# A Fourier network, windowed attention and a mixture of experts on one core: gate work moved between the expert products, and the last two spectra copied apart

## What is computed

```python
# tokens: 32 images, 64x64 pixels, 3 colours
x = coords @ fc0_w + fc0_b
for sw, cw, cb in four_layers:                       # 20 x 20 modes, 32 channels
    x1 = irfft2(einsum(rfft2(x)[:20, :20], sw))      # spectral part
    x = gelu(x1 + einsum(x, cw) + cb)                # pointwise part
h = gelu(x @ fc1_w + fc1_b) @ fc2_w + fc2_b          # (32, 64, 64)
h = concat([cls_tok, h])                             # 65 tokens of width 64
h = h + attention(layernorm(h))                      # 8 heads, window of 32
y = layernorm(h)                                     # "second norm" below
logits = y @ gate_w.T                                # 64 experts
top, idx = top_k(logits, 6); scores = softmax(top)
lattice = sum_k scores_k * (y @ lattice_weights[idx_k])
h = h + layernorm(y + lattice @ out_w.T + out_b) * ln_g + ln_b
```

## Time and profile before

| | us |
|---|---|
| median of 3 runs | 1065.15 (1063.59 to 1070.08) |
| the profiled execution's own time | 1065.44 |
| its span in the profile | 1063.6 |
| PE busy in the span | 962.6 (91%) |
| DVE busy in the span | 613.7 (58%) |

### The profile page before, as it was taken

How to read it: one execution, slowest core, us unless ns; L and a number is a source line. 1 busy time by engine, 2 the same in 40 slices (tenths; PEclk the granted TensorE clock), 3 DMA queues, 4 the chain that set the end, 5 groups by cost and what they waited for, 6 DMA issues and landing times.

```text
span 1063.6 us, 36547 instructions
## 1 busy us (share of the span) xinstructions
PE 962.6 (91%) x17004; PEld 619.0 (58%) x17004; DVE 613.7 (58%) x771; ACT 397.5 (37%) x524; POOL 152.4 (14%) x160
## 2 busy tenths in 40 slices
PE   4899999989989998999899999989888799678896
PEld 3576666656756633566567657657415587633343
DVE  2267457726844322477358548733244577768997
ACT  1333323233223387232233323223695567421200
POOL 6000000000000000000000000020000575325432
PEclk9999999999999999999999999999999899869999
DMA  6220131022011400410220031020011000000000
GB/s 197 97 79 3 40 109 30 4 94 80 3 65 49 143 5 12 121 50 3 95 80 3 15 122 40 3 95 18 2 24 47 1 2 2 1 1 1 1 7 16
DMA packets 25931, 46.78 MB, mean 44 GB/s; under 512 B 9962, under 2 KB 11013, under 8 KB 25138
## 3 DMA queue, kind: packets, MB, share of 16 engines
q1 hardware_dynamic: 24131, 42.47, 12.9%
q0 software_dynamic: 1456, 1.63, 0.6%
q10 hardware_dynamic: 192, 0.33, 0.1%
HBM read 30.25 MB, written 10.89 MB: 39 GB/s over the span
## 4 chain that ended last, share of the span: by engine, by line
PE 71%; DVE 13%; issue 5%; ACT 4%; DMA 2%; POOL 2%; SPq 1%; DVEq 0%; POOLq 0%
PE PSALL L1363 22%; PE PSALL L1331 8%; PE PSALL L1222 5%; PE PSALL L1354 5%; PE PSALL L1306 4%; PE PSALL L1236 4%; PE PSALL L550 3%; DVE WORK L1577 3%; PE PSALL L449 3%; DVE WORK L1064 2%; PE PSALL L1421 2%; DVE WORK L1596 2%; PE PSALL L536 2%; PE PSALL L1199 2%; PE PSALL L1350 2%
## 5 line engine op out<-in xcount | busy, mean ns | idle before, releaser
L1596 DVE STREAM_TRANSPOSE WORK<-PSALL 128x1024 f32<-128x1024 f32 x128 | 152.5, 1230 | 251.4 <-PE PSALL L1331 251.4
L1363 PEld LDWEIGHTS PSALL<-EW,WORK 128*64 128x64 f32 x4096 | 221.8, 138 | 72.8 <-issue 48.3
L1363 PE MATMUL PSALL<-EW,WORK 128*64 128x128 f32 x4096 | 247.6, 276 | 14.0 <-DVE WORK L1596 13.8
L1496 ACT ACTIVATE X<-PSALL,TABLES 128x1024 f32<-128x1024 f32 x128 | 141.8, 1114 | 306.5 <-PE PSALL L1363 306.5
L1577 DVE STREAM_TRANSPOSE WORK<-PSALL 128x1024 f32<-128x1024 f32 x84 | 104.3, 1242 | 32.7 <-PE PSALL L1222 30.9
L347 POOL DMA_DIRECT2D WORK<-MIXED x32 | 17.6, 550 | 666.0 <-ACT MIXED L1487 555.6
L1478 ACT COPY SPEC<-PSALL 128x400 f32<-128x400 f32 x64 | 54.0, 850 | 139.1 <-PE PSALL L1236 132.8
L1236 PEld LDWEIGHTS PSALL<-TABLES,WORK 128*64 128x64 f32 x2000 | 67.5, 139 | 47.4 <-DVE WORK L1577 31.4
L1064 DVE TENSOR_TENSOR WORK<-PSALL,X 128x910 f32<-128x910 f32 (+1 forms) x80 | 79.4, 1018 | 16.0 <-PE PSALL L536 14.4
L1236 PE MATMUL PSALL<-TABLES,WORK 128*64 128x64 f32 x2000 | 81.1, 228 | 7.5 <-DVE WORK L1577 3.9
L1530 ACT ACTIVATE WORK<-PSALL,B 128x1024 f32<-128x1024 f32 x64 | 68.2, 1114 | 8.3 <-PE PSALL L1421 7.3
(11 more groups left out here) (165 smaller groups left out, 1150.4 us busy)
## 6 DMA issues: line engine op xcount, KB each, us to landing
SW<-in_spec_w SPq DMA_DIRECT2D x160, 80.0 KB, 2.7
spec_scr<-MIXED SPq DMA_DIRECT2D x24, 400.0 KB, 3.2
SPEC<-spec_scr SPq DMA_DIRECT2D x32, 200.0 KB
WORK<-spec_scr SPq DMA_DIRECT2D x16, 200.0 KB
WORK<-in_coords_w SPq DMA_DIRECT2D x2, 1024.0 KB, 4.8
XC<-in_coords_c SPq DMA_DIRECT2D x2, 1024.0 KB, 7.1
WORK<-MIXED SPq DMA_DIRECT2D x40, 40.0 KB
WORK<-MIXED POOLq DMA_DIRECT2D x32, 40.0 KB
```

The source lines that it names most:

```text
L1363: m = pe.matmul(PS[2 * p + z][64 * j:64 * j + 64, 2 * b * GRID:(2 * b + 2) * GRID], G[:, n % 2, b, h:h + 2, :, t].rearrange("p q o -> p (q ...
L1496: nc.scalar.activation(X[:, n].rearrange("p b (z d) c w -> p d z b (c w)", z=2)[:, p, :, :, 2 * t * GRID:2 * (t + 1) * GRID], PSALL[:, 2 * ...
L1596: nc.vector.transpose(G[:, n % 2, 2 * x + y].rearrange("p h o v -> p o h v"), PSALL[:, 4 + 2 * x:6 + 2 * x, :].rearrange("p k (h o v) -> p ...
```

## The change

It has two parts that don't touch.

**The tail.** The loop has 44 steps in place of 52. Gate rows and logits of chunks 2 and 3 stay at steps 34 and 38 but go through bank 7 (before: banks 0 and 1), so rows of chunk 2 and 3 now wait for the residual that reads bank 7; those of chunks 4 to 7 stand in the expert stage after pairs 3, 5, 15 and 18 (logits one pair later). The second norm of block 2 stops at its centring (step 31); its variance stands at step 41 and its last three steps at pairs 0 and 1. The norm of block 3 starts at steps 42 and 43 and goes on at pairs 3, 4, 7 and 8. Both score chunks of block 0 are turned at step 41, each into a pair of banks of its own; `low_part(1)` goes from POOL to the DVE. PARTS3 moves to other memory and LG's blocks are rotated by one, for room. Ten products that nothing reads (`SPARE_PRODUCTS`, 128x512, bank 5) stand in PE's program: one each at steps 37, 38 and 39, two at 40 and five at 41, behind the score rows. The deviation (ACT's square root) of block 2 stands at step 41, that of block 3 behind the logits of chunk 5.

**The forward parts.** In each of the six, the eighth copy is split. Image 14's spectrum goes to one bank and is copied by ACT (`last_spectrum`, 128x200) while image 15 is still on its way; image 15's goes to the other bank and is copied by the DVE (128x200). `rows` of image 15 waits for the copy of round 6, which frees that bank; `mix()` waits for both.

The diff, cut to its core:

```diff
-ROWS_AT, CHOICE_AT, PARTS_AT = 26, 32, 40
-TAIL_STEPS = 52
+ROWS_AT, CHOICE_AT, PARTS_AT = 26, 32, 41
+TAIL_STEPS = 44
+ROWS_PAIRS = [3, 5, 15, 18]
+for i, k, s in ((29, 2, 0), (30, 2, 1), (31, 2, 2), (41, 2, 5), (41, 2, 6), (42, 3, 0), (43, 3, 1), (43, 3, 2)):
+    NORM_STEPS.setdefault(i, []).append((k, s))
+NORM_PAIRS = {0: [(2, 8), (2, 9)], 1: [(2, 10)], 3: [(3, 5)], 4: [(3, 6)], 7: [(3, 8), (3, 9)], 8: [(3, 10)]}
+SPARE_PRODUCTS = {37: 1, 38: 1, 39: 1, 40: 2, 41: 5}
...
             def gate_rows(c):
-                if c == 0:
-                    pe.wait_ge(pj_ready, (ROWS_AT - 5) // BC)
...
+                if c < 4:
+                    pe.wait_ge(pj_ready, (ROWS_AT - 5) // BC + c)
+                elif c == 4:
+                    pe.wait_ge(pj_ready, NC)
+                    pe.wait_ge(o_ready, NC)
+                elif c == 6:
+                    pe.wait_ge(rest_ready, 4)
...
-                        pe.wait_ge(lg_ready, min((i - ROWS_AT) // BC + 1, 2))
+                        pe.wait_ge(lg_ready, min((i - ROWS_AT) // BC + 1, 4))
...
-                if i in (PARTS_AT, PARTS_AT + 2):
-                    score_rows((i - PARTS_AT) // 2)
-            pe.wait_ge(gt_ready, NC)
-            pe.wait_ge(lg_ready, NC)
+                if i == PARTS_AT:
+                    score_rows(0)
+                    score_rows(1)
+                for s in range(SPARE_PRODUCTS.get(i, 0)):
+                    pe.matmul(PS[5], ident[:], TABLES[:, :, 0:128], start=True, stop=True)
...
                 if n >= 4:
                     expert_products(n - 4)
+                if n // 2 in ROWS_PAIRS:
+                    gate_rows(4 + ROWS_PAIRS.index(n // 2))
+                if n // 2 - 1 in ROWS_PAIRS:
+                    gate_logits(4 + ROWS_PAIRS.index(n // 2 - 1))
...
+                if i == PARTS_AT:
+                    high_part(0)
+                    high_part(1)
+                    middle_part(0)
+                    middle_part(1)
+                    deviation(1, 2)
             exp_logits(1)
+            gate_rows_out(4)
+            gate_logits_out(4)
+            gate_rows_out(5)
+            gate_logits_out(5)
+            deviation(1, LK - 1)
...
                 for n in range(0, NZ * PAIRS, 2):
                     z = n // PAIRS
+                    if n % PAIRS == 0:
+                        dve.wait_ge(gt_ready, slice_chunks(z))
...
+                    for k, step in NORM_PAIRS.get(n // 2, []):
+                        second_norm(k, step)
...
-                m = dft_rows(l, spec_bank[r % 2], k % 2 * SPW, Z[k % 4])
+                if k == GIMG - 1:
+                    turn.wait(sp_ready, r)
+                    m = dft_rows(l, spec_bank[0], 0, Z[k % 4])
+                else:
+                    m = dft_rows(l, spec_bank[r % 2], k % 2 * SPW, Z[k % 4])
                 if k % 2:
                     m.then_inc(sp_full.sem, 1)
+                elif k == GIMG - 2:
+                    m.then_inc(late_full.sem, 1)
...
+            def last_spectrum():
+                cols.wait(late_full, 1)
+                nc.scalar.copy(last_image(0), spec_bank[1][:, 0:SPW].rearrange("p (n r) -> p n r", r=RI)).then_inc(sp_ready.sem, 1)
...
+                    turn.wait(sp_full, ROUNDS)
+                    nc.vector.tensor_copy(last_image(1), spec_bank[0][:, 0:SPW].rearrange("p (n r) -> p n r", r=RI)
+                                          ).then_inc(final_ready.sem, 1)
```

More of the change, by code:

```diff
@@ L672, in tail_scalar @@
                     turn_out(act, (i - LAG - 2) // BC)
-                if LN_STEP + 7 <= i < LN_STEP + 7 + LK * LB and (i - LN_STEP - 7) % LB == 0:
-                    deviation(1, (i - LN_STEP - 7) // LB)
+                if i in (LN_STEP + 7, LN_STEP + LB + 7):
+                    deviation(1, (i - LN_STEP) // LB)
                 if rows_step(i - 1) is not None:
@@ L979, in rest, with second_norm @@
                     dve.wait_ge(high_ready, c + 1)
-                    nc.vector.tensor_tensor(REST[0:2 * EH, :, t], PSALL[0:2 * EH, 6:8, 0:CT], PARTS3[0:2 * EH, :, t], ALU.subtract
+                    nc.vector.tensor_tensor(REST[0:2 * EH, :, t], PSALL[0:2 * EH, part_banks(c):part_banks(c) + 2, 0:CT], PARTS3[0:2 * EH, :, t], ALU.subtract
                                             ).then_inc(rest_ready, 1)
+                def second_norm(k, step):
+                    a = slice(k * LB, (k + 1) * LB)
+                    if step == 0:
+                        dve.wait_ge(pj_ready, (k + 1) * LB // BC)
+                        nc.vector.reduce_sum(st[:, 0, a], H[:, a], AX.X).then_inc(sum_ready, 1)
+                    if step == 1:
+                        dve.wait_ge(sum_ready, k + 1)
+                        nc.vector.tensor_scalar(st[:, 0, a], st[:, 0, a], 1.0 / GRID, None, ALU.mult).then_inc(mean_ready, 1)
+                    if step == 2:
+                        dve.wait_ge(mean_ready, k + 1)
+                        nc.vector.tensor_tensor(TMP[:, a], H[:, a], over(st[:, 0, a]), ALU.subtract).then_inc(centred, 1)
+                    if step == 5:
+                        dve.wait_ge(squared, LK + k + 1)
+                        nc.vector.reduce_sum(st[:, 1, a], Y[:, a, 1, :], AX.X).then_inc(square_sum_ready, 1)
+                    if step == 6:
+                        dve.wait_ge(square_sum_ready, k + 1)
+                        nc.vector.tensor_scalar(st[:, 1, a], st[:, 1, a], 1.0 / GRID, EPS, ALU.mult, ALU.add).then_inc(var_ready, 1)
+                    if step == 8:
+                        dve.wait_ge(dev_ready, LK + k + 1)
+                        nc.vector.reciprocal(st[:, 3, a], st[:, 2, a]).then_inc(inverse_ready, 1)
+                    if step in (9, 10):
+                        dve.wait_ge(inverse_ready, k + 1)
+                        at = slice(k * LB + (step - 9) * BC, k * LB + (step - 8) * BC)
+                        nc.vector.tensor_tensor(Y[:, at], TMP[:, at].unsqueeze(2).broadcast_to([TOK, BC, 2, GRID]),
+                                                st[:, 3, at].unsqueeze(2).unsqueeze(3).broadcast_to([TOK, BC, 2, GRID]), ALU.mult
+                                                ).then_inc(half_ready if step == 9 else y_ready, 1)
                 for i in range(TAIL_STEPS):
@@ L1026, in tail @@
+                    for k, step in NORM_STEPS.get(i, []):
+                        second_norm(k, step)
                     if i == CHOICE_AT - 1:
                         dve.wait_ge(ho_out.sem, PASSES * ho_out.stride)
-                        link(nc.vector.memset(LG[:, :, EXPERTS:LW], SENTINEL))
+                        link(nc.vector.memset(LG[:, LB:NIMG, EXPERTS:LW], SENTINEL))
+                    if i == NIMG + 1:
+                        link(nc.vector.memset(LG[:, 0:LB, EXPERTS:LW], SENTINEL))
@@ L1029, in tail @@
                     if CHOICE_AT <= i <= CHOICE_AT + 8:
                         choice(0, i - CHOICE_AT)
[L1031 to L1032 removed]
+                    if i == PARTS_AT:
+                        rest(0)
+                        rest(1)
+                    if i == PARTS_AT + 2:
+                        low_part(nc.vector, dve, 1)
                 def add_projection(c):
@@ L1258, in forward @@
                 rows(l, GIMG - 1)
+                cols.wait(final_ready, 1)
             def first_columns_dft():
@@ L1507, in layer @@
                 if l:
-                    for r in range(ROUNDS):
+                    for r in range(ROUNDS - 1):
                         spectrum(r, spec_bank)
+                    last_spectrum()
+                    cols.next()
                 mixed(p, l)
```

124 lines of the change are left out of this document (55 added, 69 removed).

## The result

Twelve executions of the changed kernel had a median of 1059.06 us (1056.92 to 1063.45); twelve of the kernel before, 1065.7 (1062.45 to 1070.08). The ratio is 0.994, with a 95% interval of 0.9924 to 0.9956: 4.7 to 8.1 us faster, 6.4 in the middle. Five of the twelve of before took 1067.7 to 1070.1 us and the others at most 1066.3, while of the changed kernel one took more than 1061. The forecast was 11.1 us faster. The profiled execution had 1058.19 us in place of 1065.44.

The account below looks back on a forecast made before the run. It took the DVE to bound slice 0, PE from 1008 us on, and the DVE's chain the drain; -2.6 - 11.1 + 2.6 = -11.1 us from 1065.44 gave 1054.3 us, range 1051.5 to 1058.5.

Parts of the forecast that it names:

- The forward parts, -2.6: Ends of the six forward parts: a DVE copy of 0.40 us replaces ACT's 0.83, saving 0.43 six times, 2.6 us.
- ACT's half is hidden: Forward parts: image 14's copy runs during image 15's transpose and rows, taking less than 0.83 us against a 1.45 us lead.
- What follows is PE's own work and moves up whole: Behind the forward parts' copy: the DVE is idle there, nothing is delayed, so the full 2.6 us is kept.
- The drain, -11.1: Up to the expert stage's first multiplication: it starts at 933.6 against 944.71, 11.1 us earlier, with the spare products ending last.
- the clock falls all the same: Rival, drain: the first spare comes too late, PE runs 3 to 4 us at half pace, 1.8 us later, 1056.1; chance 0.20.
- its own sign of being wrong: Drain and pairs: first broadcast waiting for the DVE's low part, granted clock 0.50 in the spares, or DVE waits in pairs 0 to 9.
- The expert stage, +2.6: Slice 0: norm work adds 3.6 us to the DVE, less a closed 0.94 us hole: 2.6 us later at pair 10.
- the hole at pair 10 closes: Expert stage: the DVE's 0.94 us wait for PE at pair 10 disappears, reducing the added 3.6 us to 2.6.
- the new waits of PE and ACT: Expert stage: gate rows, logits and deviations fall into holes or idle time and are ready before needed, at no cost.
- The slower rival: Rival: the clock falls at 922.7 and isn't given back; eight pairs at half clock give 1068.2 us; chance 0.03.
- The rival of the longer chain: Rival, slice 0: holes move along (4.9 in place of 2.6) and new ACT or PE waits take 1.5: 1058.1; chance 0.14.

Follow-up runs that it names:

- dense copy: Changed kernel, but the DVE's copy of image 15's spectrum writes into a dense tile, not the scattered places of SPEC; one execution of 1056.59 us.
- tail alone: The changed tail with the forward parts of the kernel before; 1061.72 us, ratio 0.9968 to the kernel before.
- norm at pair 0: Changed kernel, but the last multiplication of block 2's norm stands at pair 0, not pair 1; ratio 0.9921 to the kernel before.
- early norm, two products: Changed kernel with block 2's last norm multiplication at pair 0 and two unread 128x512 products behind the broadcasts of pair 2; ratio 0.992 to the kernel before.
- fillers: Changed kernel with one more unread 128x256 product at the end of steps 35 and 36 each, where PE waits; ratio 0.9938 to the kernel before.

## Why the prediction was off

It said -2.6 - 11.1 + 2.6 = -11.1. In the trace the same three terms are -2.0, -9.4 and +4.0, with 0.3 less behind the pairs: -7.7, inside the measured 4.7 to 8.1. Which instructions get shorter and which longer was right; three sizes were not, all to the same side, and one cost was put at nothing. The largest step that failed is the clock in the drain, 1.7 us; then the norm's multiplications, 1.4, the fall of the clock behind the forward parts, some 1.3, and the DVE's copy, 0.6.

**The forward parts, -2.6.** The DVE's copy was taken at 0.40, from a dense row, and is 0.49; six holes give 0.34 each, 2.0. The prediction had written down the better number itself: ACT pays 0.34 for the scatter, and so would the DVE. The Trainium skill ("SBUF — State Buffer", section "Door 1: The DMA port swizzle") says that each access to a new 16-byte line pays. The dense copy shows the trace agrees: 0.37 against 0.49. By it, the estimate was 0.53 and 1.8 us, nearer than the forecast. That ACT's half is hidden held. "What follows is PE's own work and moves up whole" did not: in ten of eleven executions a fall of the clock came with the new forward parts, at 428 us or in the last heads, and the two columns gave 0.7 us in the mean. The prediction had no term for it.

**The drain, -11.1.** The sums from `not_equal` to the first multiplication came out right to 0.03 us where the clock held: forecast 933.6 less 921.29, 12.31 us; measured 12.34 and 12.33. Its parts were less exact: `thrice_scores` took 1.82 us, not 2.6, for before it had run beside POOL's `square`, and that gain of 0.8 vanished behind the spare products, which set the start of the score rows, as the prediction said of PE. What failed is the choice between the forecast and the rival "the clock falls all the same", priced at +1.8 and given 0.20: it came in five of the six profiled executions that have this drain unchanged: four times at +1.6 (after, tail alone, norm at pair 0, dense copy), once at +3.2 (early norm, two products). The row for it was there: the prediction saw that before the clock fell only 0.7 us behind the place of the first spare, after PE had been busy 1.86 of 3 us, and still took the spares to be in time. So its own sign of being wrong came: a granted clock of 0.50 in the spares. The first multiplication was 11.3 us earlier than before in the profile and not 13.7, and that of pair 10 7.3 and not 11.1. The work that held the clock stands in the waits before, as the fillers do. The Trainium skill ("TensorE: Matmul & The Clock Gate", Part 1) says that what the clock gate looks at is not tied to the kernel's start, so that the same kernel warms up at another place from run to run. The two executions of the changed kernel agree: 0.71 and 0.59 in one drain, 1.00 in the other.

**The expert stage, +2.6.** It cost 4.0. The norm work was sized at 0.6 us for each multiplication; two of four took 1.80 and 0.94 where they met POOL, and the others 0.69: 1.11 + 0.25 more, 1.4 in all. The early norm gave back the 1.11 (20.01 to 18.90). The rows of before already showed such waits: two L1023 in 3.06 us beside POOL's low part, and `thrice_scores` at 2.6 against 1.82. POOL of the kernel before, beside that:

```profile
925.77 1.42 POOL L733 TENSOR_TENSOR X<-X 65x512 f32<-65x512 f32 x1 [2.45 <-DVE X L1010]
```

The Trainium skill ("GPSIMD Engine Reference", section "1. Specifications") lists POOL's access to SBUF as shared with VectorE, with contention for DVE instructions with two SBUF inputs. The trace agrees: the longer instructions here all have two, and one engine waits for the other, whichever came second. Where the DVE came second it ended 0.55 us behind POOL's pass. Where POOL came second its pass grew: two records of `thrice_scores` took 3.42 us at that place in the kernel after, with a DVE multiplication of 0.69 between them, and 2.90 with the norm at pair 0, where the DVE waited instead. That the hole at pair 10 closes held, and the new waits of PE and ACT, costed at nothing, cost nothing: between 934.5 and 948.5 us the DVE waits for no other engine.

**What the prediction left out** is that the first pairs may run at half clock in spite of 9 us of full work before them. PE waits 0.89 and 1.76 us for the DVE at the first two pairs (kernel after), and the clock fell there in some executions. It is hidden while the DVE's norm work is longer (20.09 with 6.8 us at half clock, 20.01 with none). It cost 2.2 us with the fillers (22.23), where the clock was low from 6.4 to 13.2 us behind the first multiplication and not from 3.9 to 10.7, and 2.8 with the norm at pair 0 (21.71), where less norm work covered it. Some half of either was not PE itself but the 1.29 us of the multiplication that had slid onto POOL's `thrice_scores`. The slower rival (1068.2) rested on this mechanism but needed the clock to stay low from 922.7 on, which no execution of the changed tail showed. The rival of the longer chain, 1058.1, is close to the measured time by luck: no wait of ACT's or PE's came on top.

**Together**: 1054.3 + 0.6 + 1.7 + 1.4 = 1058.0, less 0.3 behind the pairs: 1057.7; with the 1.4 of the slow clock in the heads 1059.1. The profiled execution had 1058.19. Chance made it 2.28 shorter at the start, where no clock below 1.00 is recorded and the cause is open, and 0.99 longer in attention; the last 0.4 are in the forward parts and in what the device time adds to the span. The last 1.3 us between the 7.7 of the terms and the 6.4 of the times are thus about what the fall behind the forward parts takes back. That this holds in the executions that weren't profiled isn't shown, and the five long ones of the kernel before enter the 6.4 too, so the agreement to a tenth is partly luck. Nor was it settled what decides whether the clock comes back early or late at the pairs. The range left the result out by half a microsecond (1058.5 against 1059.06), because the sizes that were off were added to different rivals, each alone, and no case held them together.

## What to carry to other kernels

Size a moved DVE instruction by what will run beside it, not by its row: one with two inputs in SBUF that meets POOL's elementwise work waits for the end of POOL's pass, here up to 2.9 times its length (1.98 against 0.69), and the place of a 0.6 us step by one pair was worth 1.1 us. Products that keep PE's clock up belong into the waits before it falls, and no more of them than end before the next real input comes: each beyond that is path. Try the change without them first: here the best placing was worth 0.8 us of drain, the one chosen nothing. And cut the span at the same instructions in several executions before reading a difference of two: here 2 to 3 us came and went in stretches that the change didn't touch, and part of it turned out to come with the change after all.

## What the hardware showed unexpectedly

- The granted clock of one and the same program fell at different places: 3.4 us at half clock in the drain and 10.2 in attention in one execution, none and 17.1 in the next, with the same waits of 0.68 and 0.46 us ahead of the drain's spares.
- A fallen clock lengthens its own cure: five spares took 6.99 us mostly at half clock against 4.53, and the first multiplication came 14.55 us behind `not_equal`, where with no spares at all it came after 12.00.
- A DVE multiplication of 65x512 with two SBUF inputs took 0.69 us alone and 0.73 to 1.98 where it met a POOL pass, always ending 0.55 us (once 0.62) behind that pass, while `thrice_scores` on the DVE (65x768, twice) went from 1.82 to 2.66 beside one POOL pass of 1.42.
